# Graph attention over 50,000 edges: the loop lags of a block's sections go from at most five to at most three

## The chip, the cores and the metric

The kernel runs on one core of a Trainium2 chip. The metric is the device time of one execution in microseconds (us). Engines: PE (matrix products), DVE (elementwise on vectors, scans), ACT (activations and copies), POOL (here: indirect DMAs), SP (here: plain DMAs).

## The reference

Four layers of a graph network on 3125 nodes with 128 features and 50,000 edges, each followed by a residual sum and a layer norm. The edges are sorted by destination node. The change touches the edge part of the fourth layer, an attention with 8 heads of 16 features:

```python
ke = k[src] + e                       # e = edge_attr * We
alpha = jnp.einsum('ehd,ehd->eh', q[dst], ke) / jnp.sqrt(jnp.asarray(d, x.dtype))
m = jax.ops.segment_max(alpha, dst, num_segments=n)
m = jnp.where(jnp.isfinite(m), m, 0.0)
ex = jnp.exp(alpha - m[dst])
denom = jax.ops.segment_sum(ex, dst, num_segments=n)
w = ex / jnp.maximum(denom[dst], 1e-16)
agg = jax.ops.segment_sum(w[:, :, None] * (v[src] + e), dst, num_segments=n)
```

## The kernel before

Six stages run one after the other, with a barrier between them: `prepare`, `front`, `layers`, `middle`, `edges_attention`, `tail_nodes`. The stage of interest is `edges_attention`. The edges, padded to 392 tiles of 128, are worked off in 56 blocks of seven tiles (TB = 7, NB = 56). Every engine runs a list of *sections*, and each section does its part of one block. The sections of a block n, in the order in which its data flow:

- SP `index` loads the sources' numbers; POOL `gather` (L1766) issues seven indirect DMAs, one a tile, that fetch key and value rows into `e_kv`, of which there are eight buffers (KS). Gathers of block n wait until `message` of block n - 8 is done (`exv`).
- SP `load` brings the destinations (`e_drow`, two buffers), the queries at segment starts (`e_qs`, four) and the segment heads (`e_dh`).
- ACT `masks` (L1818, L1821) builds 128 x 128 masks of equal destinations, `e_mask`.
- PE `fill` (L1780): mask times `e_qs` puts each edge's query into PSUM, `e_q`. There is one such buffer, so it waits for `scores` of block n - 1. The seven products are recorded as 14 matmuls.
- DVE `scores` (L1883 to L1891): products with the keys, sum by head, the edge term: `e_al`.
- PE `turn` (L1787) transposes `e_al` into `e_a`; DVE `breaks` (L1875, L1877) prepares segment borders, DVE `maxima` (L1867, L1870) runs a forward and a backward scan, `e_fs` and `e_bs`; PE `back` (L1794) transposes `e_bs` into `e_m`.
- DVE `differ` (L1859, L1861): `e_dif` = `e_al` - `e_m`, and a copy of the maxima to the output row.
- ACT `exp` (L1826), DVE `message` (L1850, L1852): weights times values, `e_msg` (two buffers).
- PE `total` (L1801): mask times `e_msg`, sums by destination into `e_p` (one buffer, 14 matmuls); ACT `evac` (L1832, L1833) copies it to `e_row`; ACT `store` (L1839) sends it to memory.

The helper `pipelined` (L78) writes an engine's program: in each turn of the loop it calls the sections in the order of the list, and a section with lag g works on the block of this turn minus g. The lags shape each engine's own queue alone; between engines only semaphores count, so what matters is which block's sections stand beside each other on one engine and in which order. The first sixteen turns (`head=2`) are written out, the rest is a loop of eight turns. The engines' queues are in order: what stands behind a section that waits, waits too.

Of the kernel before, what the change touches and what calls it, by code (L numbers as in the profile page):

```python
# [22 lines left out]
NB = 56  # L23
# [11 lines left out]
KS = 8  # L35
# [42 lines left out]
def pipelined(eng, count, slots, sections, head=1):  # L78

    deepest = max(lag for lag, _ in sections)
    assert deepest <= slots and count % slots == 0
    for step in range(head * slots):
        for lag, do in sections:
            if step >= lag:
                do(step - lag, (step - lag) % slots, (step - lag) // slots)
    with eng.Fori(head, count // slots) as i:
        for k in range(slots):  # L90
            for lag, do in sections:
                do(i * slots + (k - lag), (k - lag) % slots, i + (k - lag) // slots)
    for step in range(count, count + deepest):
        for lag, do in sections:
            if step - lag < count:
                do(step - lag, (step - lag) % slots, (step - lag) // slots)
# [58 lines left out]
def gnn_kernel(nc, xp, srccol, dstcol, dstflat, dsthead, lasthead, headtail, wcol, edgesT, wmat, wrow, wbc, gvec, out):  # L155
    ctx = ExitStack()
    with ctx:
# [1505 lines left out]
        def edges_attention():  # L1663
            with ExitStack() as st:
# [25 lines left out]
                def in_bank(ps, t, width):  # L1690

                    at = t // PT * BANK + t % PT * width
                    return ps[:, at:at + width]
# [6 lines left out]
                def one(ps, width, lo, hi):  # L1700

                    return in_bank(ps, TM, width)[:, lo:hi]

                def by_bank(a):

                    return a[:, 0:TM, :].rearrange("p (b t) f -> p b t f", t=PT)
# [13 lines left out]
                def heads(a):  # L1720
                    return a.rearrange("p (t h) -> p t h", h=H)

                with nc.Block() as block:
                    @block.sync
                    def _(sp):
                        c.credit(sp)
                        with nc.allow_non_contiguous_dma(reason="five numbers per edge tile"):
                            sp.dma_start(firsts[:, :], headtail[:, :, 4]).then_inc(first_in, 16)

                        def index(n, s, r):  # L1730
                            if not (isinstance(r, int) and r == 0):
                                wait_rows(sp, s, r - 1, TB)
                            c.hold(sp)
                            with nc.allow_non_contiguous_dma(reason="seven sources per partition"):
                                sp.dma_start(idx[s][:, :], srccol[:, bass.ds(n * TB, TB)]).then_inc(indexed[s], 16)

                        def load(n, s, r):
                            c.free(sp, "mask", n, 2)
                            c.hold(sp)
                            sp.dma_start(drow[s][:, :, :].rearrange("p t e -> p (t e)"),  # L1740
                                         dst_short[bass.ds(n * BW, BW)].partition_broadcast(P)).then_inc(landed[s], 16)
                            c.free(sp, "fq", n, ES)
                            sp.wait_ge(first_out, 16)
                            c.hold(sp)
                            sp.dma_start(qs[s][:, :, :], flat_rows(q_starts, n)).then_inc(landed[s], 16)
                            c.free(sp, "brk", n, ES)
                            c.hold(sp)
                            sp.dma_start(dh[s][:, :], dsthead[bass.ds(n * HR, HR), :]).then_inc(landed[s], 16)

                        pipelined(sp, NB, KS, [(0, index), (4, load)])  # L1750
                        for s in range(KS):
                            sp.wait_ge(stored[s], NB // KS * 16)
# [18 lines left out]
                    @block.tensor  # L1771
                    def _(pe):
                        def fill(n, s, r):

                            c.ready(pe, "mask", n)
                            pe.wait_ge(landed[s], (r + 1) * 48)
                            c.free(pe, "prod", n, 1)
                            c.free(pe, "wq", n, 1)
                            for t in range(TB):
                                last = nc.tensor.matmul(in_bank(ps_q, t, QW), mask[s][:, t, :], qs[s][:, t, :], start=True, stop=True)  # L1780
                            last.then_inc(c["fq"], 1)

                        def turn(n, s, r):
                            c.ready(pe, "al", n)
                            c.free(pe, "fs", n, 1)
                            c.hold(pe)
                            nc.tensor.transpose(ps_a[0:HR, 0:P], al[s][:, :], ident[:, :]).then_inc(c["at"], 1)  # L1787

                        def back(n, s, r):
                            c.ready(pe, "bs", n)  # L1790
                            c.free(pe, "dif", n, 1)
                            c.free(pe, "m", n, 1)
                            c.hold(pe)
                            nc.tensor.transpose(ps_m[:, 0:HR], bs[s][:, :], ident[0:HR, 0:HR]).then_inc(c["mt"], 1)  # L1794

                        def total(n, s, r):
                            c.ready(pe, "exv", n)
                            c.ready(pe, "exw", n)
                            c.free(pe, "evp", n, 1)
                            for t in range(TB):  # L1800
                                last = nc.tensor.matmul(in_bank(ps_p, t, MW), mask[s][:, t, :], msg[s][:, t, :], start=True, stop=True)  # L1801
                            last.then_inc(c["p"], 1)

                        pipelined(pe, NB, KS, [(4, total), (2, back), (0, fill), (1, turn)])

                    @block.scalar
                    def _(act):
                        act.preload_act_table_set("exp_and_others")
                        nc.scalar.activation(neg_dst[:, :], dst_i[:, :], ACT.Copy, scale=-1.0).then_inc(negated, 1)
                        act.wait_ge(negated, 1)  # L1810
                        act.wait_ge(picked, 16 * TK)
                        act.dma_start(q_starts[0:EP, :].rearrange("(k p e) f -> p k e f", e=P, p=TP)[:, :, 0, :], qfirst[:, :, :]).then_inc(first_out, 16)

                        def masks(n, s, r):
                            act.wait_ge(landed[s], (r + 1) * 48)
                            c.free(act, "p", n)
                            for t in range(TB):
                                last = nc.scalar.activation(mask[s][:, t, :], drow[s][:, t, :], ACT.Abs, bias=neg_dst[:, bass.ds(n * TB + t, 1)])  # L1818
                            last.then_inc(c["off"], 1)
                            c.ready(act, "off", n)  # L1820
                            nc.scalar.activation(mask[s][:, :, :], mask[s][:, :, :], ACT.Relu, scale=-1.0, bias=ones[:, 0:1]).then_inc(c["mask"], 1)  # L1821

                        def exp(n, s, r):
                            c.ready(act, "dif", n)
                            c.free(act, "p", n, RS)
                            nc.scalar.activation(msg[s][:, :, D:D + H], heads(dif[s][:, :]), ACT.Exp).then_inc(c["ex"], 1)  # L1826

                        def evac(n, s, r):

                            row_free(act, s, r)  # L1830
                            c.ready(act, "p", n)
                            nc.scalar.activation(by_bank(row[s])[:, :, :, 0:MW], many(ps_p, MW, 0, MW), ACT.Copy)  # L1832
                            nc.scalar.activation(row[s][:, TM, 0:MW], one(ps_p, MW, 0, MW), ACT.Copy).then_inc(c["evp"], 1)  # L1833

                        def store(n, s, r):
                            c.ready(act, "evp", n)
                            c.hold(act)
                            c.ready(act, "m", n)
                            act.dma_start(flat_rows(sums_att, n), row[s][:, :, :]).then_inc(stored[s], 16)  # L1839

                        pipelined(act, NB, KS, [(0, masks), (4, exp), (5, evac), (5, store)], head=2)

                    @block.vector
                    def _(dve):
# [45 lines left out]
                            c.free(dve, "dif", n, ES)  # L1890
                            dve.tensor_tensor(al[s][:, :], red[s][:, :], wq[s][:, :], ALU.add).then_inc(c["al"], 1)  # L1891

                        pipelined(dve, NB, KS, [(4, message), (3, differ), (2, maxima), (0, breaks), (1, scores)], head=2)
            count_rows(KS, NB, TB)


# [352 lines left out]
```

## Time and profile before

| what | value |
|---|---|
| median of 3 runs | 2227.64 us (2219.5 to 2228.99) |
| the profiled execution's own time | 2228.31 us |
| its span, first to last instruction | 2226.6 us |
| mean granted TensorE clock over the span | 0.785 of full speed |
| busy share of the span | PE 61%, DVE 48%, ACT 42%, POOL 47% |
| attention stage: first `fill` to last `store` | about 1441 to 2124 us of the span |

The profile names an instruction by engine, line, operation and tensors without their buffer numbers: `e_msg` is `e4_msg0` and `e4_msg1`. "x14" is a count of like instructions merged into one row. In brackets stands how long the engine sat idle before the row and what released it; "remote" and "issue" are releasers that the trace can't name, and a semaphore that an earlier stage used under another name carries that name (`x_now<-in_xp`). PEclk is the granted clock of PE as a share of full speed: 0.50 is 1.2 GHz, 1.00 is 2.4 GHz.

### The profile page before, as it was taken

The page shows a single profiled execution, that of the slowest core. Times are in us where ns is not written, and L with a number is a line of the kernel's source. Part 1 is how long each engine was busy: PE and PEld are TensorE (multiplying, and loading weights), DVE is VectorE, ACT ScalarE, POOL GpSimd, SP SyncE. Part 2 cuts the span into 40 slices and gives each one's busy share as a digit, 9 for nine tenths or more (in the row PEclk, how much of TensorE's full clock was granted, in tenths as well). Part 3 has the DMA queues.
Part 4 walks back from the last instruction along what each step waited for, and adds up shares of the span by engine and source line. Part 5 has one row for each costly group of instructions (what it writes and reads, how often), then busy time and mean ns, then how long its engine had stood idle before and what let it go on. Part 6 is the DMA issues. An engine that isn't in the chain of part 4 may idle for free. (4 is left out here: it accounts for less than half of the span.)

```text
span 2226.6 us, 31431 instructions
## 1 busy us (share of the span) xinstructions
PE 1354.5 (61%) x7918; PEld 1101.4 (49%) x7918; DVE 1067.3 (48%) x2945; ACT 943.8 (42%) x2003; POOL 1046.1 (47%) x1184
## 2 busy tenths in 40 slices
PE   4412236766667789699989996314454454444567
PEld 2200014434455568599989994214344443434555
DVE  4411149874344467555964215214344444434666
ACT  0100137774444568275526645313333333334324
POOL 5577710004666640024558342674655566565233
PEclk9555559888888899999989997657667677667886
DMA  4222212224555563074545451555666666665521
GB/s 148 62 68 52 67 59 89 104 95 152 164 174 178 185 208 101 13 257 158 187 159 206 146 184 52 149 143 160 190 191 173 187 193 188 188 175 174 168 62 37
DMA packets 214478, 314.19 MB, mean 141 GB/s; under 512 B 31638, under 2 KB 160149, under 8 KB 214224
## 3 DMA queue, kind: packets, MB, share of 16 engines
q1 hardware_dynamic: 111130, 153.97, 21.8%
q0 software_dynamic: 33488, 81.02, 13.0%
q10 hardware_dynamic: 69734, 77.65, 10.9%
q8 instruction: 64, 1.05, 0.2%
q14 instruction: 62, 0.51, 0.1%
HBM read 223.87 MB, written 88.67 MB: 140 GB/s over the span
## 5 line engine op out<-in xcount | busy, mean ns | idle before, releaser
L372 POOL DMA_INDIRECT fr_ring<-table,src_i x392 | 374.9, 956 | 412.7 <-SPq L649 277.4
L1766 POOL DMA_INDIRECT e_kv<-kv_table,e_idx x392 | 388.0, 990 | 262.0 <-DVE e_msg L1852 146.4
L679 PE MATMUL fe_ps<-fe_space 128*128 128x400 bf16 x591 | 175.9, 424 | 243.9 <-issue 153.4
L679 PEld LDWEIGHTS fe_ps<-fe_space 128*128 128x128 bf16 x591 | 86.1, 146 | 333.1 <-issue 307.5
L770 DVE TENSOR_SCALAR fe_space<-fe_space,fr_key 128x400 bf16<-128x400 f16 x591 | 159.0, 325 | 173.6 <-remote 64.8
L1801 PE MATMUL e_p<-e_msg,e_mask 128*128 128x144 f32 x784 | 141.4, 346 | 146.8 <-issue 103.8
L998 POOL CAST ly_af<-ly_au 128x640 fp32r<-128x640 uint16 x240 | 163.2, 726 | 127.4 <-DVE ly_part L1403 61.1
L1801 PEld LDWEIGHTS e_p<-e_msg,e_mask 128*128 128x128 f32 x784 | 130.7, 240 | 159.8 <-issue 139.5
L1780 PE MATMUL e_q<-e_qs,e_mask 128*128 128x136 f32 x784 | 148.2, 360 | 87.4 <-issue 62.4
L725 ACT ACTIVATE fe_space<-fe_ps 128x800 uint16<-128x800 f32 x100 | 83.5, 835 | 257.9 <-PE fe_ps L679 167.4
L1832 ACT ACTIVATE e_row<-e_p 128x864 f32<-128x864 f32 x56 | 49.5, 884 | 334.4 <-remote 292.3
L701 PE MATMUL fe_ps<-fr_ring,fe_space 128*128 x976 | 147.2, 292 | 62.7 <-issue 33.9
L1780 PEld LDWEIGHTS e_q<-e_qs,e_mask 128*128 128x128 f32 x784 | 135.5, 258 | 94.2 <-issue 88.6
L701 PEld LDWEIGHTS fe_ps<-fr_ring,fe_space 128*128 128x128 f32 x976 | 129.2, 203 | 70.6 <-issue 70.6
L1064 PE MATMUL ly_ps<-ly_af,ly_x_high 128*128 128x256 f32 (+1 forms) x650 | 160.2, 288 | 2.4 <-POOL ly_af L998 2.4
L1818 ACT ACTIVATE e_mask<-e_drow,e_neg_dst 128x128 f32<-128x128 uint16 x392 | 120.6, 388 | 89.5 <-issue 41.9
L1064 PE MATMUL ly_ps<-ly_af,ly_x_low 128*128 128x256 f32 (+1 forms) x650 | 156.5, 282 | 0.0
L688 PEld LDWEIGHTS fe_ps<-wm,fe_edge 128*128 128x128 f32 x784 | 114.8, 210 | 61.0 <-issue 59.0
L685 PE MATMUL fe_ps<-fr_ring,ident 128*128 128x512 f32 x196 | 114.8, 670 | 48.6 <-DVE fr_ring L818 38.2
L735 ACT ACTIVATE fe_space<-fe_space 128x512 f32<-128x512 f32 x98 | 61.4, 627 | 175.4 <-DVE fe_space L813 158.7
L1867 DVE TENSOR_TENSOR_SCAN e_fs<-e_brk,e_a 56x128 f32<-56x128 f32 x56 | 22.9, 409 | 218.0 <-remote 176.1
L1064 PEld LDWEIGHTS ly_ps<-ly_af,ly_x_high 128*128 128x128 f32 x650 | 125.0, 192 | 3.3 <-POOL ly_af L998 2.6
(396 smaller groups left out, 3068.4 us busy)
## 6 DMA issues: line engine op xcount, KB each, us to landing
ly_au<-edge_counts SPq DMA_DIRECT2D x88, 800.0 KB, 4.6
sums_att<-e_row ACTq DMA_DIRECT2D x56, 532.0 KB
q_starts<-fe_space SPq DMA_DIRECT2D x56, 476.0 KB
e_qs<-q_starts SPq DMA_DIRECT2D x56, 476.0 KB
fe_edge<-in_edgesT ACTq DMA_DIRECT2D x98, 256.0 KB
edge_counts<-fe_space ACTq DMA_DIRECT2D x25, 800.0 KB
e_drow<-dst_short SPq DMA_DIRECT2D x56, 224.0 KB
fr_ring<-table,src_i POOLq DMA_INDIRECT x392
```

The source lines that it names most:

```text
L372: pool.indirect_dma_start(f.ring[:, n % RB, t, 0:D], None, tab[0][:, :], bass.IndirectOffsetOnAxis(ap=src_i[:, at:at + 1].bitcast(U32), ax ...
L679: nc.tensor.matmul(ps[:, bass.ds(at, NW)], left(n), right(n % IS), start=False, stop=True, skip_group_check=True).then_inc(c["item"], 1)
L685: nc.tensor.matmul(bank_of(n), ident[:, :], ring[:, n % RB, :, 0:D], start=True, stop=True)
L688: last = nc.tensor.matmul(bank_of(n)[:, t * P:(t + 1) * P], edge[n % ER][:, t * P:(t + 1) * P], wm[:, W_E, :], start=False, stop=True, ski ...
L701: last = nc.tensor.matmul(sum_of(i), hot_n(i % NH)[:, t, :], flat[:, bass.ds(at + t * RW1, D + 1)], start=(t == 0), stop=(t == TF - 1))
L770: dve.tensor_scalar(right(s), numbers, f.key[:, bass.ds(n, 1)], None, ALU.is_equal).then_inc(c["hot"], 1)
L998: part_in = pool.tensor_copy(counts_of(m)[:, a:a + NS, :], au[at_load(m) % AS][:, a:a + NS, :])
L1064: nc.tensor.matmul(ps_a[g % 2][:, 0:width(g)], piece[:, a, :], af[:, g % AF, 0:len(tiles(g)), a, :], start=(a == 0 and k == 0), stop=False)
L1766: pool.indirect_dma_start(kv[s][:, t, :], None, kv_table[:, :], bass.IndirectOffsetOnAxis(ap=idx[s][:, t:t + 1].bitcast(U32), axis=0)).the ...
L1780: last = nc.tensor.matmul(in_bank(ps_q, t, QW), mask[s][:, t, :], qs[s][:, t, :], start=True, stop=True)
L1801: last = nc.tensor.matmul(in_bank(ps_p, t, MW), mask[s][:, t, :], msg[s][:, t, :], start=True, stop=True)
L1818: last = nc.scalar.activation(mask[s][:, t, :], drow[s][:, t, :], ACT.Abs, bias=neg_dst[:, bass.ds(n * TB + t, 1)])
```

## The change

Only the lists of sections on PE, ACT and DVE change: their lags and, on PE and DVE, their order.

```diff
--- before.py
+++ after.py
@@ -1801,7 +1801,7 @@
                                 last = nc.tensor.matmul(in_bank(ps_p, t, MW), mask[s][:, t, :], msg[s][:, t, :], start=True, stop=True)
                             last.then_inc(c["p"], 1)
 
-                        pipelined(pe, NB, KS, [(4, total), (2, back), (0, fill), (1, turn)])
+                        pipelined(pe, NB, KS, [(2, turn), (2, back), (3, total), (1, fill)])
 
                     @block.scalar
                     def _(act):
@@ -1838,7 +1838,7 @@
                             c.ready(act, "m", n)
                             act.dma_start(flat_rows(sums_att, n), row[s][:, :, :]).then_inc(stored[s], 16)
 
-                        pipelined(act, NB, KS, [(0, masks), (4, exp), (5, evac), (5, store)], head=2)
+                        pipelined(act, NB, KS, [(0, masks), (2, exp), (3, evac), (3, store)], head=2)
 
                     @block.vector
                     def _(dve):
@@ -1890,7 +1890,7 @@
                             c.free(dve, "dif", n, ES)
                             dve.tensor_tensor(al[s][:, :], red[s][:, :], wq[s][:, :], ALU.add).then_inc(c["al"], 1)
 
-                        pipelined(dve, NB, KS, [(4, message), (3, differ), (2, maxima), (0, breaks), (1, scores)], head=2)
+                        pipelined(dve, NB, KS, [(2, scores), (3, message), (2, maxima), (1, breaks), (2, differ)], head=2)
             count_rows(KS, NB, TB)
```

On PE, in the written-out turns. Before, one turn from `fill` to `fill`: block 5 is filled, `turn` serves block 4 (`e4_al0`), `total` block 2, `back` block 4, and then block 6 is filled.

```order
L1780 MATMUL e4_q<-e4_qs1,e4_mask5 128x136 x7
L1787 MATMUL e4_a<-ident,e4_al0 56x128
L1801 MATMUL e4_p<-e4_msg0,e4_mask2 128x144 x7
L1794 MATMUL e4_m<-ident,e4_bs0 128x56
L1780 MATMUL e4_q<-e4_qs2,e4_mask6 128x136 x7
L1787 MATMUL e4_a<-ident,e4_al1 56x128
L1801 MATMUL e4_p<-e4_msg1,e4_mask3 128x144 x7
L1794 MATMUL e4_m<-ident,e4_bs1 128x56
L1780 MATMUL e4_q<-e4_qs3,e4_mask7 128x136 x7
```

Now, from the `fill` of block 5:

```order
L1780 MATMUL e4_q<-e4_qs0,e4_mask4 128x136 x7
L1787 MATMUL e4_a<-ident,e4_al0 56x128
L1794 MATMUL e4_m<-ident,e4_bs0 128x56
L1801 MATMUL e4_p<-e4_msg1,e4_mask3 128x144 x7
L1780 MATMUL e4_q<-e4_qs1,e4_mask5 128x136 x7
L1787 MATMUL e4_a<-ident,e4_al1 56x128
L1794 MATMUL e4_m<-ident,e4_bs1 128x56
L1801 MATMUL e4_p<-e4_msg0,e4_mask4 128x144 x7
L1780 MATMUL e4_q<-e4_qs2,e4_mask6 128x136 x7
```

`turn` and `back` after a `fill` of block 5 both serve block 5 (`e4_al1`, `e4_bs1`), `total` serves block 4, and only then comes the `fill` of block 6. Before, `total` stood between the `turn` and the `back` of a block, and the `fill` behind them served a block two further on.

On DVE, from the sum of the scores of one block to the first product of the next. Before:

```order
L1888 TENSOR_REDUCE e4_red1<-e4_prod0 128x56
L1891 TENSOR_TENSOR e4_al1<-e4_red1,e4_wq1 128x56
L1850 TENSOR_TENSOR e4_msg1<-e4_msg1,w_col 128x7x8
L1852 TENSOR_TENSOR e4_msg1<-e4_kv7,e4_msg1 128x7x128
L1859 TENSOR_TENSOR e4_dif0<-e4_al0,e4_m 128x56
L1861 COPY e4_row0<-e4_m 128x7x8
L1867 SCALAR_TENSOR_TENSOR e4_fs1<-e4_brk1,e4_a 56x128
L1870 SCALAR_TENSOR_TENSOR e4_bs1<-e4_brk1,e4_fs1 56x128
L1875 TENSOR_TENSOR e4_brk3<-e4_dh3 56x129
L1877 TENSOR_SCALAR e4_brk3<-e4_brk3 56x129
L1883 TENSOR_TENSOR e4_prod0<-e4_q,e4_kv2 128x768
```

Now:

```order
L1888 TENSOR_REDUCE e4_red3<-e4_prod0 128x56
L1891 TENSOR_TENSOR e4_al3<-e4_red3,e4_wq3 128x56
L1850 TENSOR_TENSOR e4_msg0<-e4_msg0,w_col 128x7x8
L1852 TENSOR_TENSOR e4_msg0<-e4_kv6,e4_msg0 128x7x128
L1867 SCALAR_TENSOR_TENSOR e4_fs3<-e4_brk3,e4_a 56x128
L1870 SCALAR_TENSOR_TENSOR e4_bs3<-e4_brk3,e4_fs3 56x128
L1875 TENSOR_TENSOR e4_brk0<-e4_dh0 56x129
L1877 TENSOR_SCALAR e4_brk0<-e4_brk0 56x129
L1859 TENSOR_TENSOR e4_dif3<-e4_al3,e4_m 128x56
L1861 COPY e4_row3<-e4_m 128x7x8
L1883 TENSOR_TENSOR e4_prod0<-e4_q,e4_kv0 128x768
```

Before, behind the scores that use `e4_al1` come the messages of a block two behind (`e4_kv7` under scores of buffer 1), the differences of the block before (`e4_al0`) and the scans of this one, then `breaks` and the next scores. Now the messages are those of the block just before, the scans come right behind them, `breaks` next, and the differences of the same block (`e4_al3`) last, in front of the next block's scores. On ACT the section order stays; `exp` comes two blocks behind the masks, where it was four, and the copy and the store three, where it was five.

## Rows read from the trace of the kernel before

**Rows 1.** Windows view: us of stretch; busy time (instructions) of each engine; PEclk; DMA share; GB/s
```profile
1515.00:2079.00 564.00, 261.08 (x1422) 235.50 (x1421) 240.86 (x658) 204.57 (x516) 333.70 (x335) 0.70 0.66 185
2079.00:2125.00 46.00, 31.69 (x199) 27.88 (x197) 33.06 (x90) 21.52 (x51) 0.00 (x0) 0.88 0.48 136
```

**Rows 2.** Waits view, 1455 to 2126 us: us in total, times, longest
```profile
POOL e_kv L1766 <- DVE e_msg L1852: 146.4, 19, 14.7
...
DVE e_prod L1883 <- remote: 12.3, 1, 12.3
...
ACT e_row L1832 <- remote: 292.3, 23, 25.4
```

**Rows 3.** Timeline: start us, us, engine line op out<-in [idle before <-releaser]; one burst of gathers
```profile
1585.43 0.95 POOL L1766 DMA_INDIRECT e_kv<-kv_table,e_idx  x1 [8.92 <-DVE e_msg L1852]
...
1585.93 3.02 PE L1801 MATMUL e_p<-e_msg,e_mask 128*128 128x144 f32 x14
...
1589.05 0.89 ACT L1832 ACTIVATE e_row<-e_p 128x864 f32<-128x864 f32 x1 [4.00 <-PE e_p L1801]
...
1590.80 0.27 PE L1787 MATMUL e_a<-ident,e_al 128*56 128x128 f32 x1
...
1591.16 1.98 PE L1801 MATMUL e_p<-e_msg,e_mask 128*128 128x144 f32 x14
...
1593.98 0.41 DVE L1867 TENSOR_TENSOR_SCAN e_fs<-e_brk,e_a 56x128 f32<-56x128 f32 x1 [2.63 <-remote]
...
1598.41 0.27 PE L1787 MATMUL e_a<-ident,e_al 128*56 128x128 f32 x1
...
1608.25 0.89 ACT L1832 ACTIVATE e_row<-e_p 128x864 f32<-128x864 f32 x1 [14.18 <-remote]
...
1611.40 0.95 POOL L1766 DMA_INDIRECT e_kv<-kv_table,e_idx  x1 [0.30 <-issue]
...
1615.35 0.41 DVE L1867 TENSOR_TENSOR_SCAN e_fs<-e_brk,e_a 56x128 f32<-56x128 f32 x1 [5.43 <-remote]
```

**Rows 4.** Timeline of DVE after the last gather, one turn
```profile
2094.74 0.94 DVE L1883 TENSOR_TENSOR e_prod<-e_q,e_kv 128x768 f32<-128x768 f32 x1
...
2097.36 1.09 DVE L1852 TENSOR_TENSOR e_msg<-e_kv,e_msg 128x896 f32<-128x896 f32 x1
...
2099.04 0.42 DVE L1870 TENSOR_TENSOR_SCAN e_bs<-e_brk,e_fs 56x128 f32<-56x128 f32 x1
```

**Rows 5.** Timeline of PE, `fill` (L1780) and `total` (L1801) at both clocks
```profile
1582.41 3.51 PE L1780 MATMUL e_q<-e_qs,e_mask 128*128 128x136 f32 x14 [1.36 <-DVE e_wq L1886]
...
1618.05 3.51 PE L1780 MATMUL e_q<-e_qs,e_mask 128*128 128x136 f32 x14 [1.36 <-DVE e_wq L1886]
...
1621.57 2.28 PE L1801 MATMUL e_p<-e_msg,e_mask 128*128 128x144 f32 x14
...
1624.51 1.86 PE L1780 MATMUL e_q<-e_qs,e_mask 128*128 128x136 f32 x14 [0.46 <-issue]
...
1626.79 1.98 PE L1801 MATMUL e_p<-e_msg,e_mask 128*128 128x144 f32 x14 [0.31 <-issue]
...
1633.83 3.51 PE L1780 MATMUL e_q<-e_qs,e_mask 128*128 128x136 f32 x14 [1.45 <-issue]
...
1645.18 3.70 PE L1801 MATMUL e_p<-e_msg,e_mask 128*128 128x144 f32 x14 [7.62 <-issue]
```

**Rows 6.** Timeline, the first and the last blocks of the stage
```profile
1497.41 0.42 DVE L1870 TENSOR_TENSOR_SCAN e_bs<-e_brk,e_fs 56x128 f32<-56x128 f32 x1
...
1497.97 0.32 PE L1794 MATMUL e_m<-ident,e_bs 56*128 56x56 f32 x1 [37.09 <-DVE e_bs L1870]
...
1512.18 1.08 DVE L1852 TENSOR_TENSOR e_msg<-e_kv,e_msg 128x896 f32<-128x896 f32 x1
...
2118.70 1.08 DVE L1852 TENSOR_TENSOR e_msg<-e_kv,e_msg 128x896 f32<-128x896 f32 x1
...
2124.34 0.38 ACTq L1839 DMA_DIRECT2D sums_att<-e_row  x1
```

## The prediction

> **What bounds the kernel now.** The change touches one stage, the attention over 56 blocks of seven edge tiles, so I read that stage alone. First the windows view: from the stage's 60th us or so to its last gather no engine is full; in 564 us PE is busy 46%, DVE 43%, ACT 36%, POOL 59%, the DMA engines 66%, and the granted clock is 0.70 on average. After the last gather, with POOL quiet, the last eight blocks go through in 46 us and the clock is at 0.88 [rows 1]. So while POOL gathers, the other engines wait. The waits view says for what: POOL waits 146.4 us for DVE's message products (L1852), which set a block's key/value buffer free, and ACT waits 292.3 us in front of its copy of the sums out of PSUM, for a releaser that the view can't name [rows 2].
>
> The timeline of one cycle shows who that is. POOL gets leave for three blocks in quick order and issues 21 gathers from 1585.43 to 1612.35, so 1.28 us each and 9.0 us a block. A `total` of PE that ends at 1588.95, 3.5 us into this burst, is read by ACT at 1589.05. A `turn` that ends at 1591.07, 5.6 us in, is read by DVE only at 1593.98, 2.9 us later. The `total` that ends at 1593.14, 7.7 us in, is read at 1608.25, 15.1 us later; the `turn` that ends at 1598.68 is read at 1615.35, which is 3.0 us after the burst's last gather [rows 3]. **Results of PE reach DVE and ACT late while POOL has been gathering for more than some 5 us.** Why, no view shows; how late, the rows do. The cycle then is: three blocks pass fast, the engines stall until POOL is nearly through, then `message` frees buffers and the next burst begins. A block costs 11 us on average: from the first `message` (its end, 1513.26) to the last (2119.78) are 606.5 us for 55 steps, 11.0 each [rows 6].
>
> **The change part by part.** No instruction is added or removed; 56 blocks do what they did. What moves is which block each section works on.
>
> (1) *PE's turn* (the names of the sections are those of the code). Before, PE has `total` of block k-4, `back` of k-2, `fill` of k and `turn` of k-1 in a turn; between a result of PE and DVE's reading of it lies at least a `message` with the differences, or a whole `scores`, of another block. Now `turn` and `back` of block n stand first, then `total` of n-1, then `fill` of n+1. `back` waits for DVE's second scan of the same turn, and `fill` of the next block, which DVE needs at once, is queued behind it and behind `total`. So PE's 28 long matmuls stand after DVE's scans and before DVE's next scores, one behind the other.
>
> (2) *DVE's turn.* From the first product of the scores to the end of `message` are 3.7 us (2094.74 to 2098.45), and the second scan ends 1.0 us after that: 4.7 us [rows 4]. `breaks` and `differ` then run beside PE's `total` and cost nothing; should PE be quick, they would cost 0.8 us of idle DVE at most.
>
> (3) *The path of a turn.* From the end of the scan: `back` starts 0.14 us later and takes 0.32 [rows 6]; then `total` 1.98 and `fill` 1.86 at the full clock, 3.70 and 3.51 at half [rows 5]. A turn is 4.7 + 0.3 + 1.98 + 1.86 = 8.9 us with the full clock throughout, and 4.7 + 0.45 + 3.70 + 3.51 = 12.35 us at half. Before, DVE's own work alone set the pace of an undisturbed turn.
>
> (4) *Which clock.* In the new turn PE has 4.7 us between `fill` and `total` that hold only two small transposes. The nearest row: after a `total` that ended at 1628.77 PE had one transpose in 5.06 us, and the next `fill`, at 1633.83, took 3.51: the clock had gone to 1.2 GHz [rows 5]. It came back within the work that followed: with a `fill` from 1618.05 on, the `total` at 1621.57 took 2.28, so was slow for a sixth of its work, 4.2 us after PE had begun; with one from 1582.41 on, the `total` of 1585.93 took 3.02, slow for six tenths, 5.7 us after [rows 3, 5]. Taken together: each turn starts at half clock, `total` takes 3.70, and of `fill` a seventh to six tenths is slow, 2.1 to 2.8 us. The path is then 4.7 + 0.4 + 3.65 + 2.45 = **11.2 us a turn**.
>
> The Trainium skill (TensorE: Matmul & The Clock Gate, section "HAM oscillation — how this bites in real kernels") says that a loop in which each burst of matmuls is followed by a long enough idle stretch starts every burst at half clock, over and over. It speaks against this change: by it the turn is the 11.2 us above, and without it, at the full clock, 8.9 us. The rows agree in the one gap of this length.
>
> (5) *Late results.* The rows of before have no single burst of seven gathers. In the new turn POOL starts some 0.8 us after `message` ends and stops 9.7 us after it; `fill` ends 1.0 + 0.4 + 6.1 = 7.5 us after it, 6.7 us into POOL's burst. Ends: it may be read at once (as at 3.5 us, and as everything is once POOL is quiet), or only 3.0 us after POOL's last gather, at 12.7, so 5.2 us late [rows 3]. Below zero is excluded: DVE can't start earlier. The nearest row is the 2.9 us at 5.6 us in; but there three blocks' loads, stores and gathers fell together, and here one block's do. I take half of it, 1.4 us, and keep 0 and 5.2. The other two results of a turn are asked for while POOL is quiet (`turn`) or within 2 us of its start (`back`) and cost nothing extra.
>
> (6) *Start and end.* The first scan of block 0 ends at 1497.83 in both. Then `back` (0.46), `fill` of block 1 (3.51, at half clock), scores and `message` 3.7: the first `message` would end at 1505.5, where it ended at 1513.3 [rows 6], a gain of 7.8 us. After the last `message` 4.6 us go by until the last store is issued [rows 6]; that stays.
>
> (7) *What is moved past what.* On ACT exp, copy and store follow the masks by two and three blocks instead of four and five; ACT's turn (3.2 + 0.2 + 1.2 us of work and the issue) is far under 11 and hides. The store comes one turn earlier for the row buffer's next writer, a wait that no row shows as binding. SP's and POOL's queues are as before; the gathers have one block more of lead, worth nothing, since the only wait in front of the scores' first product, where DVE waits for a gather or a `fill`, is one of 12.3 us [rows 2], at the stage's start. On POOL the wait before a gather changes size: 56 turns of the other engines set it.
>
> **Sum.** 48 turns beside gathers at 11.2 + 1.4 = 12.6 us, seven at 11.2: 604.8 + 78.4 = 683.2. End of the stage 1505.5 + 683.2 + 4.6 = 2193.3, against 2124.3 [rows 6]: +69 us. On the profiled execution's 2228.3 that is 2297; the median of the three runs is 0.7 lower: **2296 us**. The turn at which nothing changes is (2124.3 - 1505.5 - 4.6) / 55 = 11.17 us; every tenth of a us more costs 5.5 us.
>
> **The rivals.**
> *Faster: POOL is never starved.* If PE keeps the full clock and results come on time, the turn is 8.9 us and POOL's 9.0 is the bound: 1505.5 + 48 x 9.0 + 7 x 8.9 + 4.6 = 2004.4, 120 us less, 2107. It decides from 11.1 us a turn down. For it: the bursts of three blocks are what makes results late, and an even pace would break them up; the first 5 us of a burst are undisturbed; the DMA engines at 66% have room; POOL's 146.4 us are nearly the whole gain. Against: the gap of 4.7 us. A clock that stays up in part of the turns gives 10 us and about 2165. Chance 0.27.
>
> *No change.* Half clock at each start, but no lateness: 11.2 us, 2230. Or the lateness alone sets the pace, as now, whatever the order. Chance 0.12.
>
> *Much slower.* `fill` is held until POOL is through: 3.7 + 12.7 = 16.4 us in 48 turns, +251 us, 2478. For it: the `total` that ended 7.7 us into a burst was held for 15.1 us, nearly to the burst's end, and `fill` ends 6.7 us into its own. Against: POOL stops 2 us later here, where it had 13 us to go there, and each turn moves a third of the data. Chance 0.12 for above 2400.
>
> *My forecast*, turns of 11.5 to 14.8 us, 2245 to 2400: 0.49. Since PE's results must now cross to DVE three times in a row within one turn, two of them with little or nothing to do meanwhile, it is the likeliest.
>
> **How the numbers follow.** 0.5% (11 us) is about what a measurement can tell from no change. Faster 0.27, within it 0.12, slower 0.49 + 0.12 = 0.61. The range goes from 2125 (9.3 us a turn; 0.08 of the faster case lies below) to 2400 (14.8 us; 0.12 above): 8 in 10. The forecast's own range is 2245 to 2400.
>
> **What would show it.** In the changed profile: gathers in groups of seven with a wait before each (3 to 4 us if I am right, under 1 in the faster case); DVE idle 5 us or more in front of the first product of the scores (L1883), where it now waits once; `total` of 3.7 us in most turns and a granted clock near 0.6 to 0.7; ACT's 292 us moved to `dif` and `p` of the same turn. I am wrong if the gathers stand without gaps, if `total` takes 2.0 us throughout, or if PE's results are read at once 7 us into POOL's work.

## The result, and the profile after

The changed kernel takes 2271.47 us (median of 4 runs, 2268.11 to 2275.51), the kernel before beside it 2227.69 (4 runs, 2219.5 to 2228.99): **1.020 times as long, 95% interval 1.016 to 1.024**. The forecast was 2296, in a range of 2125 to 2400. The profiled execution of the changed kernel took 2274.03 us, its span is 2272.3.

The windows view, beside the gathers and behind the last one, which ends at 2098.19 (columns as in [rows 1]):

```profile
1515.00:2115.00 600.00, 309.06 (x1453) 284.48 (x1454) 254.26 (x686) 221.26 (x539) 316.10 (x330) 0.69 0.64 178
2115.00:2170.00 55.00, 31.70 (x169) 29.04 (x167) 26.68 (x70) 17.26 (x41) 0.00 (x0) 0.81 0.24 73
```

POOL, the DMA engines and the clock read nearly as before. What is new is the second row: with POOL quiet the DMA engines move 73 GB/s where they moved 136 [rows 1], so the other engines take blocks at about half the rate. The tile view of the message products (L1852; durations in ns, then first and last start) and the timeline of DVE at the stage's end say it in times:

```profile
L1852 DVE TENSOR_TENSOR e_msg<-e_kv,e_msg x56: 1081/1084/1086, 1504.9 to 2163.7; 128x896 f32<-128x896 f32 x56
```

```profile
2120.21 1.08 DVE L1852 TENSOR_TENSOR e_msg<-e_kv,e_msg 128x896 f32<-128x896 f32 x1
...
2130.32 1.08 DVE L1852 TENSOR_TENSOR e_msg<-e_kv,e_msg 128x896 f32<-128x896 f32 x1
...
2160.66 1.08 DVE L1852 TENSOR_TENSOR e_msg<-e_kv,e_msg 128x896 f32<-128x896 f32 x1
...
2163.69 1.08 DVE L1852 TENSOR_TENSOR e_msg<-e_kv,e_msg 128x896 f32<-128x896 f32 x1
```

The same timeline of the kernel before:

```profile
2092.28 1.09 DVE L1852 TENSOR_TENSOR e_msg<-e_kv,e_msg 128x896 f32<-128x896 f32 x1
...
2097.36 1.09 DVE L1852 TENSOR_TENSOR e_msg<-e_kv,e_msg 128x896 f32<-128x896 f32 x1
```

A turn with POOL quiet takes 10.1 us now (2120.21 to 2130.32) and took 5.1 before. The last gathers start at 2097.24 and at 2077.99 (0.95 us each), so 19.3 us later than before; from the last gather's end to the last message are 65.5 us, where it was 39.8, another 25.7. Together that is the stage's 45.0 us (last message 2163.7 against 2118.7 [rows 6]). The first message comes 7.3 us earlier. So less than half of the net loss, 19.3 of 45.0 us, has arisen when the last gather is issued: 46 turns there (messages 4 to 50) took 12.20 us each, and took 11.84 before.

The waits view of the stage, 1425 to 2180 us (columns as in [rows 2]):

```profile
...
DVE e_prod L1883 <- remote: 203.3, 22, 37.6
DVE e_prod L1883 <- PE e_q L1780: 182.0, 30, 7.3
ACT e_msg L1826 <- DVE e_dif L1859: 180.0, 52, 6.2
POOL e_kv L1766 <- DVE e_msg L1852: 171.9, 43, 12.7
...
ACT e_row L1832 <- issue: 129.7, 41, 3.2
```

DVE waited once in front of the first product of the scores, for 12.3 us [rows 2]; now it waits 52 times, 385 us, for `fill` (`e_q`) or for a releaser without a name. POOL waits in 43 places instead of 19, since its gathers now come block by block, and 25 us more in all. ACT waits 193 us in front of the copy of the sums (`e_row`), 129.7 of them in 41 waits of 3.2 us at most; before, it waited 334 us there, 292.3 for the nameless releaser, which keeps 27.4. Another 234 us stand before exp (`e_msg` L1826).

One turn beside gathers, timeline of all engines (start, us, engine, line, operation, tiles, idle before it and its releaser):

```profile
1737.28 0.96 DVE L1883 TENSOR_TENSOR e_prod<-e_q,e_kv 128x768 f32<-128x768 f32 x1 [6.15 <-PE e_q L1780]
...
1739.91 1.08 DVE L1852 TENSOR_TENSOR e_msg<-e_kv,e_msg 128x896 f32<-128x896 f32 x1
...
1741.36 0.42 DVE L1870 TENSOR_TENSOR_SCAN e_bs<-e_brk,e_fs 56x128 f32<-56x128 f32 x1
...
1741.78 1.01 POOL L1766 DMA_INDIRECT e_kv<-kv_table,e_idx  x1 [2.07 <-issue]
...
1741.92 0.32 PE L1794 MATMUL e_m<-ident,e_bs 56*128 56x56 f32 x1 [1.63 <-DVE e_bs L1870]
...
1742.17 3.73 PE L1801 MATMUL e_p<-e_msg,e_mask 128*128 128x144 f32 x14
...
1745.69 2.44 PE L1780 MATMUL e_q<-e_qs,e_mask 128*128 128x136 f32 x14
...
1749.38 0.95 POOL L1766 DMA_INDIRECT e_kv<-kv_table,e_idx  x1 [0.30 <-issue]
1749.72 0.96 DVE L1883 TENSOR_TENSOR e_prod<-e_q,e_kv 128x768 f32<-128x768 f32 x1 [7.01 <-remote]
...
1754.22 1.01 POOL L1766 DMA_INDIRECT e_kv<-kv_table,e_idx  x1 [3.88 <-DVE e_msg L1852]
```

The two first products are 12.44 us apart: DVE 4.50 (to the end of its second scan at 1741.78), `back` and the crossing 0.39, `total` 3.52 up to the start of `fill`, `fill` 2.44, and then 1.59 between the end of `fill` at 1748.13 and its reading at 1749.72. POOL issued seven gathers in that time and then waited 3.88 us for `message`. Measured in the same way over the 47 turns beside gathers from the fourth on, `fill` is read 1.5 us after its end on average (at most 4.9); in the last six turns, with POOL quiet, 0.04 us after it.

The releaser without a name is `fill` itself. The trace also keeps the moments at which semaphores were updated, and the scores at 1749.72 wait for three of them: the landing of the block's gathers stands at 1681.48, DVE's own reduction at 1728.13, and `fill`'s update at 1749.70. In the kernel before it is the same: the `total` that ended at 1593.14 has its update at 1608.17, 0.08 us before ACT's copy, while the store that the copy also waits for had landed at 1560.46. PE had gone on meanwhile (`back` at 1594.99, the next `fill` at 1596.72). So neither late gathers nor late stores hold DVE and ACT up here; the signal of PE's finished work comes late.

And it comes at a time that POOL's burst sets, not a fixed time after `fill`. Two turns in a row:

```profile
1562.59 1.00 POOL L1766 DMA_INDIRECT e_kv<-kv_table,e_idx  x1 [3.12 <-DVE e_msg L1852]
...
1566.31 1.78 PE L1780 MATMUL e_q<-e_qs,e_mask 128*128 128x136 f32 x14
...
1569.76 0.96 DVE L1883 TENSOR_TENSOR e_prod<-e_q,e_kv 128x768 f32<-128x768 f32 x1 [6.33 <-remote]
...
1574.26 1.00 POOL L1766 DMA_INDIRECT e_kv<-kv_table,e_idx  x1 [3.13 <-DVE e_msg L1852]
...
1578.17 2.57 PE L1780 MATMUL e_q<-e_qs,e_mask 128*128 128x136 f32 x14
...
1581.47 0.96 DVE L1883 TENSOR_TENSOR e_prod<-e_q,e_kv 128x768 f32<-128x768 f32 x1 [6.37 <-PE e_q L1780]
```

`fill` ends 5.50 us after the burst's first gather in the first turn and 6.48 in the second, and is read at 7.17 and 7.21. In 21 of 46 turns beside gathers it is read 7.10 to 7.25 us after the first gather, with ends from 5.34 to 6.90; in 5 turns it is read earlier (5.91 at the least), in 20 later (10.46 at the most). From the end of `message` to the first gather are 0.79 us, from the first product of the scores to the end of `message` 3.71: with 7.2 between them that is a turn of 11.7 us, and the median turn takes 11.8.

### The profile page after: what moved, and what is told of

Read it like the earlier page. It is cut to its first block and busy times, and to the rows that moved or that the text cites. A ratio compares the mean times of both kernels' runs of the same rounds, so it can differ in the third digit from the quotient of the medians.

```text
span 2272.3 us, 31400 instructions
## 1 busy us (share of the span) xinstructions
PE 1400.9 (62%) x7918; PEld 1152.2 (51%) x7918; DVE 1069.7 (47%) x2945; ACT 951.0 (42%) x2003; POOL 1033.2 (45%) x1184
## 3 DMA queue, kind: packets, MB, share of 16 engines
q1 hardware_dynamic: 111130, 153.97, 21.6%
## 5 line engine op out<-in xcount | busy, mean ns | idle before, releaser
L1766 POOL DMA_INDIRECT e_kv<-kv_table,e_idx x392 | 376.0, 959 | 288.1 <-DVE e_msg L1852 171.9
L1883 DVE TENSOR_TENSOR e_prod<-e_q,e_kv 128x768 f32<-128x768 f32 x56 | 53.6, 957 | 416.1 <-remote 203.3
L1801 PE MATMUL e_p<-e_msg,e_mask 128*128 128x144 f32 x784 | 202.8, 449 | 1.3 <-ACT e_row L1833 1.3
L1787 PE MATMUL e_a<-ident,e_al 128*56 128x128 f32 x56 | 19.3, 345 | 280.4 <-issue 141.9
L1801 PEld LDWEIGHTS e_p<-e_msg,e_mask 128*128 128x128 f32 x784 | 184.9, 326 | 7.1 <-issue 1.6
L1787 PEld LDWEIGHTS e_a<-ident,e_al 128*56 128x56 f32 x56 | 6.6, 117 | 290.3 <-issue 290.3
L1780 PE MATMUL e_q<-e_qs,e_mask 128*128 128x136 f32 x784 | 129.7, 330 | 29.0 <-issue 29.0
L1780 PEld LDWEIGHTS e_q<-e_qs,e_mask 128*128 128x128 f32 x784 | 129.8, 246 | 29.8 <-issue 29.7
```

What stands on the lines that cost most here:

```text
L1766: pool.indirect_dma_start(kv[s][:, t, :], None, kv_table[:, :], bass.IndirectOffsetOnAxis(ap=idx[s][:, t:t + 1].bitcast(U32), axis=0)).the ...
```

## The experiments

The experiments ran on four chips. The kernel before takes 1716 to 1730 us on two of them (A and C below) and 2212 to 2232 on the other two (B and D). So each result is compared with the kernel before on its own chip, and the chip is named.

### `fill` ahead of `total` (chip A)

```
-pipelined(pe, NB, KS, [(2, turn), (2, back), (3, total), (1, fill)])
+pipelined(pe, NB, KS, [(2, turn), (2, back), (1, fill), (3, total)])
```

> The changed kernel with PE's order turn, back, fill, total: the fill of the next block no longer stands behind the total. My theory (a turn is DVE's 4.7 us plus back, total and fill one behind the other) gives 4.7 + 0.4 + 3.5 = 8.6 us, under POOL's 9.0, so turns of 9.0 to 9.5 us and 2271 - 55 x 2.7 = about 2120 us. The rival (results of PE come late whenever POOL gathers, whatever the order, and that sets the pace) gives turns of 11 us or more and at best 2220 us.

Measured: 1719.23 us (10 runs) against 1726.2 (13 runs), ratio 0.997 (0.995 to 0.998). The messages go from 1116.2 to 1608.9, 8.96 us a turn. Its waits:

```profile
DVE e_prod L1883 <- DMA e_kv<-kv_table,e_idx: 137.6, 34, 7.0
POOL e_kv L1766 <- issue: 119.5, 392, 0.3
```

POOL never waits for a message; it is the bound, and DVE waits for gathers. So it is `total` in front of `fill` that makes the serial path long: with `fill` first the faster rival's 9.0 us are reached, where the changed kernel takes 10.1 us on the other chip of this kind (C, below). But the kernel before takes 1726 us on this chip, so there the gain is 0.3%.

### Matmuls in PE's gap (chip A)

```
+for _ in range(8):
+    nc.tensor.matmul(ps_a[:, P:2 * P], ident[:, :], iota[:, :], start=True, stop=True)
```

behind each `fill` of the changed kernel.

> The changed kernel with 8 idle 128 x 128 products (16 matmuls, into columns of PSUM that nobody reads) behind each fill, so that PE is busy in the 4.7 us of DVE's work. Theory of the clock: total falls from 3.73 to about 2.0 us and fill to 1.86, turns from 12.0 to about 9.6 us, 2271 - 55 x 2.4 = about 2140 us. Rival (the clock is not what costs; POOL or late results set the turn): the total gets shorter, the wait behind it longer, 2260 to 2275 us. If the extra products are themselves in the way, total is short and e_a starts late behind them.

Measured: 1771.73 us (4 runs), ratio 1.027 (1.024 to 1.030). The message products (L1854 here) go from 1116.0 to 1663.9, 9.96 us a turn; `total` takes 3.27 us in the median, `fill` 2.16, so the expected 2.0 and 1.86 were missed, and the 9.6 us a turn with them. From 1150 to 1550 us, by the windows view:

```profile
1150.00:1550.00 400.00, 295.84 (x1832) 280.43 (x1832) 203.14 (x551) 179.41 (x438) 300.37 (x310) 0.84 0.82 230
```

The changed kernel has 0.79 in the same stretch (row below, on chip C) and 10.11 us a turn. Eight matmuls did not keep the clock up, so the run as a whole tells how little they give (0.15 us a turn). In two of its turns `total` took 1.98 us, its time at the full clock; they took 8.4 us each, against the 8.9 that the prediction had for the full clock.

### The old order on PE, the new on DVE and ACT (chip A)

```
-pipelined(pe, NB, KS, [(2, turn), (2, back), (3, total), (1, fill)])
+pipelined(pe, NB, KS, [(4, total), (2, back), (0, fill), (1, turn)])
```

> The lists of DVE and ACT as changed, PE's list as before (total of k-4, back of k-2, fill of k, turn of k-1). If the loss comes from PE's queue alone, fill again has a scores and a message of lead, turns are 6.6 to 9.9 us by their own path, POOL's 9.0 us is the bound and the time is 2110 to 2150 us. Rival: with fast turns the bursts of three blocks and the 15 us of late results come back, turns of 11 us on average, 2215 to 2235 us.

Measured: 1813.55 us (4 runs), ratio 1.051 (1.048 to 1.054); 10.71 us a turn (1119.1 to 1707.9). The expectation missed. Its waits:

```profile
ACT e_row L1832 <- PE e_p L1801: 311.8, 56, 9.2
PE e_q L1780 <- ACT e_mask L1821: 294.5, 53, 29.1
```

`fill` now needs the masks of its own turn, and on ACT these stand behind exp and the copy of the sums, which wait for PE. By these waits the loop is closed over ACT instead of over PE alone; no further run tested that reading. PE's order and the others' have to be changed together; one list cannot be judged by itself.

### No gathers on POOL, the old order (chips A, C and D)

In place of POOL's seven gathers SP loads seven tiles of fixed rows with one plain DMA; the waits for the rows count one DMA instead of seven.

```
-pipelined(sp, NB, KS, [(0, index), (4, load)])
+def plain(n, s, r):
+    c.free(sp, "exv", n)
+    c.hold(sp)
+    sp.dma_start(kv[s][:, :, :], kv_table[0:BW, :].rearrange("(t p) f -> p t f", p=P)).then_inc(gathered[s], 16)
+pipelined(sp, NB, KS, [(0, index), (4, load), (2, plain)])
...
-pipelined(pool, NB, KS, [(0, gather)])
```

> The kernel before, with the seven indirect gathers of a block left out on POOL; in their place SP loads the same number of bytes of the key/value table with one plain DMA (fixed rows, so keys and values are not those of the edges). The DMA traffic stays, POOL is idle. If POOL's gathering is what makes PE's results reach DVE and ACT late, no wait of 10 us and more is left in front of e_row and e_dif, and turns are 5.1 us (DVE) to 8 us (DMA): 1840 to 2010 us. If the DMA traffic, or the loads and stores of SP and ACT, are the cause, the waits of 14 us every third block stay and the time is over 2150 us.

> The kernel before with plain loads by SP in place of POOL's gathers (fixed rows, keys and values not those of the edges), once more, wanted on a chip where the kernel before takes 2220 us. If POOL's gathering is what makes PE's results late there, the bursts of waits in front of e_row and e_dif vanish and a block takes 6.0 us as on the fast chip, so about 1950 us. If the traffic does it, over 2150 us.

> The kernel before with plain loads by SP in place of POOL's gathers, still wanted on a chip where the kernel before takes 2220 us: about 1950 us there if POOL's gathering makes PE's results late and nothing else does (6.0 us a block), over 2150 us if it is the traffic. On a chip of the fast kind 1560 us, as twice before.

Measured: 1559.55 us on chip A (1 run; the kernel before 1726.2), 1566.85 on chip C (before 1725.25), 1894.4 on chip D (before 2226.68). The message products, by the tile view of the runs on chips C and D:

```profile
L1856 DVE TENSOR_TENSOR e_msg<-e_kv,e_msg x56: 1076/1084/1087, 1132.6 to 1462.1; 128x896 f32<-128x896 f32 x56
```

```profile
L1856 DVE TENSOR_TENSOR e_msg<-e_kv,e_msg x56: 1075/1084/1087, 1459.2 to 1789.5; 128x896 f32<-128x896 f32 x56
```

(1462.1 - 1132.6) / 55 = 6.0 us a turn on chip C, and 6.0 on chip D, where the kernel before takes 10.9. So without POOL's gathers the stage is the same on both kinds of chip, and the whole 327 us between the two runs lie ahead of it. Chips A and C have no late results even beside gathers (below), so only the run on chip D tells of their cause. The waits there, first of the kernel before, then of this one:

```profile
ACT e_row L1832 <- remote: 259.1, 22, 26.1
```

```profile
ACT e_mask L1822 <- DMA e_dh<-in_dsthead: 117.3, 54, 18.6
...
ACT e_row L1836 <- PE e_p L1805: 9.9, 5, 3.3
```

No wait for a nameless releaser is left, at 357 GB/s from 1500 to 1750 us, about twice the rate beside gathers. What ACT waits for is SP's loads: the 6.0 us are the pace of the transfers, and the order's own is nearer the 5.1 us that it reaches behind the last gather. On chip D removing the gathers saves 332 us of the kernel before, on chip C 158.

### Both kernels and the first experiment on chip B

> The kernel before, unchanged, once more, for its trace on the chip of the experiments, where the runs of the kernel before took 1726 us and not 2228. Theory: there no result of PE comes late while POOL gathers, POOL is the bound of the attention stage with 9.0 us a block and hardly waits for DVE (under 30 us where it was 146). Should the chip be like the first one, 2228 us and the same waits.

> The changed kernel, unchanged, once more. With results on time its turn is the path alone, 11.2 us (4.7 on DVE, back, total at half clock, fill partly so), against POOL's 9.0 before: 55 x 2.2 = 120 us more than the kernel before on the same chip, about 1845 us where before takes 1726. Rival (late results of PE were what cost): on a chip without them before and after are equal within 1%. On a chip like the first, 2271.

> PE's order turn, back, fill, total with the changed lists of DVE and ACT, once more, to stand beside the changed kernel on one chip. Theory of the queue: turns of 9.0 us, POOL's bound, so 1720 us on a chip like the last one; on a chip like the first one fill ends 5 us after message and is read on time, 2130 us.

Measured on chip B: the kernel before 2220.28 us (7 runs), and 2212.09 in the run with a profile (10.93 us a turn); the changed kernel 2250.66 (4 runs), ratio 1.014 (1.009 to 1.019), 11.71 us a turn; `fill` ahead of `total` 2248.72 (4 runs), ratio 1.013 (1.008 to 1.018), 11.67 us a turn. So the loss repeats, a little smaller than in the result, and the order that reached 8.96 on chip A gains nothing here: its expectation of 2130 us was missed, and the rival of the first experiment (at best 2220 us, whatever PE's order) holds on this chip. By stretches, the changed kernel ends its last gather 2.0 us later than the kernel before and takes 65.9 us from there to its last message, where the kernel before takes 31.6: nearly the whole loss lies where POOL is quiet. With `fill` first the last gather ends 21.6 us later than in the kernel before, and 47.3 us follow it. So the shorter path pays behind the last gather, and beside the gathers late results take it back. The timeline of one of its turns shows how:

```profile
1705.63 3.34 PE L1780 MATMUL e_q<-e_qs,e_mask 128*128 128x136 f32 x14
...
1708.80 1.88 PE L1801 MATMUL e_p<-e_msg,e_mask 128*128 128x144 f32 x14
...
1711.47 0.95 POOL L1766 DMA_INDIRECT e_kv<-kv_table,e_idx  x1 [0.30 <-issue]
1714.97 0.96 DVE L1883 TENSOR_TENSOR e_prod<-e_q,e_kv 128x768 f32<-128x768 f32 x1 [8.98 <-remote]
1715.18 0.89 ACT L1832 ACTIVATE e_row<-e_p 128x864 f32<-128x864 f32 x1 [6.22 <-remote]
...
1719.47 1.01 POOL L1766 DMA_INDIRECT e_kv<-kv_table,e_idx  x1 [7.05 <-DVE e_msg L1852]
...
1723.51 0.96 DVE L1883 TENSOR_TENSOR e_prod<-e_q,e_kv 128x768 f32<-128x768 f32 x1 [3.19 <-PE e_q L1780]
```

`fill` ends at 1708.97 and is read at 1714.97, 6.0 us later and 2.55 us after the last gather; `total` ends at 1710.68 and is read at 1715.18. The next turn is short: its first product stands 8.54 us behind this one, which stood 16.15 us behind the one before. POOL waits 24 times here, so a burst serves two blocks or so; and the second of a burst pays. That is the pattern of the kernel before [rows 3], with bursts of two for bursts of three. Here too POOL sets the moment: in 19 turns `fill` is read 19.9 to 20.2 us after the first gather of the burst (1695.02 for this one), with ends from 12.1 to 14.9.

### No gathers on POOL, the new order (chip B)

The same edit as above, made in the changed kernel.

> The changed kernel with the seven indirect gathers of a block left out on POOL; SP loads as many bytes of the key/value table with one plain DMA (fixed rows, so keys and values are not those of the edges). Theory: the path of a turn holds without POOL too, 11.2 us, so the stage takes as long as in the changed kernel, or on a chip with late results 0.8 us a turn less. Rival (POOL is part of what slows the changed kernel): turns of 8 us or less, 170 us less or more.

Measured: 2117.63 us (1 run); its message products go from 1453.6 to 2011.2, 10.14 us a turn. Its timeline (all lines 4 higher):

```profile
1703.34 3.43 PE L1805 MATMUL e_p<-e_msg,e_mask 128*128 128x144 f32 x14
...
1706.56 2.05 PE L1784 MATMUL e_q<-e_qs,e_mask 128*128 128x136 f32 x14
...
1708.65 0.96 DVE L1887 TENSOR_TENSOR e_prod<-e_q,e_kv 128x768 f32<-128x768 f32 x1 [4.86 <-PE e_q L1784]
...
1718.76 0.96 DVE L1887 TENSOR_TENSOR e_prod<-e_q,e_kv 128x768 f32<-128x768 f32 x1 [4.85 <-PE e_q L1784]
```

`fill` ends at 1708.61 and is read at 1708.65. `fill` is read at most 0.23 us after its end in any turn, though the DMA engines carry more than beside the gathers: 216 GB/s from 1500 to 1950 us, where the changed kernel has 178 in the result. So **the late results go with POOL's gathering, not with the traffic** (one run in each order, on chips D and B; whether POOL's issuing or the fetching of scattered rows is what counts they don't separate), and the path without them is 10.1 us: 4.1 us longer than the old order's 6.0 on the same kind of chip, which the transfers set.

### The changed kernel on chip C, the one before on chip D

> The changed kernel, unchanged, once more, wanted on a chip where the kernel before takes 1726 us. The changed kernel with plain loads took 10.1 us a turn with every result read at once, so that is its path; POOL's bound is 9.0. On the fast chip: 55 x 1.1 = 60 us over the kernel before, about 1786 us. Rival (late results are the whole loss): 1726 us within 1%. On a chip with late results 2250 to 2275 us.

> The kernel before, unchanged, for its trace, wanted on a chip of the fast kind. There POOL bounds the attention stage: 9.0 us from message to message, POOL hardly waits for DVE (under 50 us in all where it was 146), no wait for a result of PE is longer than 3 us. On a chip of the slow kind 2220 us and the bursts as known.

Measured: the changed kernel 1783.96 us (4 runs) against 1725.25 (7 runs), ratio 1.035 (1.032 to 1.038). The kernel before was profiled on chip D: 2221.22 us, with the waits and late results as known. No profile of it exists where it takes 1726. The waits of the changed kernel on chip C, and its windows view:

```profile
DVE e_prod L1883 <- PE e_q L1780: 276.3, 56, 6.3
```

```profile
1150.00:1550.00 400.00, 226.72 (x1170) 209.82 (x1170) 202.57 (x550) 176.80 (x433) 298.15 (x306) 0.79 0.83 227
```

All 56 waits are for `fill`, none for a nameless releaser; POOL waits 20.1 us for messages in the whole stage. A turn takes 10.11 us (1120.5 to 1676.8), as without gathers, and POOL's gathers beside it change nothing on this chip. Nothing but the serial path is left to cost the 3.5% here. Were all of the 58.7 us lost in these 55 turns and at the start (7 us gained, as in the result), the kernel before would have turns of 10.11 - (58.7 + 7) / 55 = 8.9 us, POOL's own pace. That is worked out, not seen.

## Why the prediction was right, and where its sizes were off

**Step 1, the serial path, held.** `fill` and `total` stand one behind the other between DVE's second scan and its next scores in every turn of the profile. Where results come on time, the turn is 10.1 us (chip C), and 9.0 with `fill` first (chip A). Where they come late (chip B), this order shortens nothing but the turns behind the last gather.

**Step 2, DVE's 4.7 us, is 4.5.** The price was read from [rows 4], where the differences and the copy (L1859, L1861) still stood between `message` and the scans. The order lists said that they move behind; the sum kept them in.

**Steps 3 and 4, the clock, held in kind.** `total` takes 3.73 us in the median turn, where it takes 1.98 at the full clock [rows 5]: the 1.2 GHz level after a gap that holds only two transposes. `fill` behind it was forecast at 2.45 and takes 2.2 in the median, 2.33 on average beside gathers; and two neighbouring groups of matmuls lie 0.2 us over each other in the rows, which the sum of their durations does not take off. The forecast path was 11.2 us; it measures 10.1 without gathers, and about 10.7 beside them in the result's profile (12.20 less 1.5). The Trainium skill (TensorE: Matmul & The Clock Gate, section "HAM oscillation — how this bites in real kernels") has a loop of short bursts and long idle stretches start every burst slow. The trace agrees for `total`: but for the stage's last one, none of the 56 takes less than 3.26 us. It does not show the whole turn at that level: the granted clock is 0.79 with results on time, and 0.69 with the late ones.

**Step 5, late results: 1.5 us a turn against 1.4, and partly by luck.** The bound of 5.2 was not exceeded from the fourth turn on (4.9), and 0.04 with POOL quiet is the other end; while POOL issues the stage's first gathers a `fill` is read 35.9 us late. But half of one row's 2.9 us was a guess, and the term isn't what the step took it for. It adds a delay to the end of `fill`, while the rows show `fill` held until a moment of POOL's burst. So beside the gathers `message`, burst, release and scores make the turn (0.8 + 7.2 + 3.7 us), and the steps on PE count only where they outlast the 7.2. It follows that a quicker PE would have gained little there; that is argued, and the order with `fill` first on chip B, which gained nothing beside the gathers, speaks for it. What the step did not say either is that the kernel before pays as much in another way, and that the two come out nearly alike: 11.84 and 12.20 us a turn beside gathers.

**Step 6.** The first message ended at 1505.96, forecast 1505.5. From the last message's end to the last store are some 6.4 us (2164.8 to 2171.2), forecast 4.6.

**The sum** was 69 us and is 45. The 55 steps from message to message were forecast at 683.2 us and took 658.8. Of the 24.4 us between them 9.5 lie in the 48 steps beside the gathers (595.3 against 604.8) and 14.9 in the seven behind them: six took 10.1 instead of 11.2, which makes 6.7, and the last took 3.0 instead of 11.2, which makes 8.2. The sum overlooked that no scores stand in front of the last message. Against the kernel before, the stretch behind the last gather makes 25.7 of the 45 us, where the forecast's own numbers had 78.4 less the old 39.8, so 38.6 of 69. Up to there the loss is 26.6 us, and the earlier start takes 7.3 off.

**The rivals.** POOL's 9.0 us a turn were never reached by this change; by the first experiment they are what PE's other order gives on chip A. "No change" was wrong by the condition of its first half, since lateness is there; its second half, lateness alone setting the pace, is near what the rows show beside the gathers, and it left out the stretch behind them. "Much slower", with every `fill` held until POOL is through, does not occur in the changed kernel: at 1749.72 the scores start while POOL's last gather runs. It does occur with bursts of two blocks, above.

**What stays open.** How POOL's gathering holds back the signals of PE's results was not found. The Trainium skill (GPSIMD Engine Reference, section "1. Specifications") has VectorE and GpSimd share their way to SBUF, with contention for DVE instructions of two SBUF inputs. The message products are of that form, and take 1.08 us beside gathers (1739.91) as with POOL quiet (2120.21); so it is not this work of DVE that is held up, it starts late. Nor was it found why two chips show no lateness and two do.

## What to carry to other kernels

Fewer turns between a block's start and end mean that its results cross engines back to back; before closing a loop over several engines, add up the chain from one engine's last result to its next start, and ask whether the longest piece in it (here `total`, 3.5 us) is needed there or only happens to be queued there. When one engine waits for another, check whether the wait grows with the other's work or ends at a moment that a third one sets: here the ends of `fill` lie up to 1.6 us apart, and it is read at the same 7.2 us of POOL's burst. Look at the stretch where the suspected bound is quiet: a turn of 5.1 against 10.1 us shows there at once, and a crowded stretch hides it. And run a pair of kernels on more than one chip before ranking two orders: here one order gains 0.3% on one chip and loses 1.3% on another.

## What the runs showed of the hardware

The same program takes 1725 to 1726 us on chips A and C and 2220 to 2228 on B, D and that of the result. The difference begins in the first stage, which gathers on POOL too. The gathers of that stage, tile view, changed kernel in the result and on chip C:

```profile
L372 POOL DMA_INDIRECT fr_ring<-table,src_i x392: 942/945/1582, 19.8 to 804.8; - x196
```

```profile
L372 POOL DMA_INDIRECT fr_ring<-table,src_i x392: 944/946/1582, 20.2 to 539.4; - x196
```

Each gather's issue takes the same 0.95 us, but the 392 of them are spread over 785 us instead of 519. On B, D and the result's chip the signal of a result of PE may stand in the trace 6 us after its end while POOL gathers (15 in [rows 3], 35.9 at the stage's start in the changed kernel), at a moment that goes by POOL's burst: in 21 of 46 turns 7.10 to 7.25 us after the first of seven gathers (result's chip), in 19 turns 19.9 to 20.2 after the first gather of a longer burst (chip B); on A and C the waits views of the stage have no wait for a nameless ("remote") releaser at all. With the attention's gathers replaced by plain loads the old order runs at 6.0 us a turn on A, C and D alike; the new one runs at 10.1 so on B, as it does with its gathers on C.
